# A graph kernel: four buffers in place of three for adjacency tiles, four in place of two for row loads, and a new order of the steps

## What is computed

```
h = max(layernorm(x), 0)
x = x + (A / clip(sum(A, axis=2), 1)) @ h            # layer 0: weighted mean over neighbors
h = max(layernorm(x), 0)
neigh = (A > 0) without the diagonal;  rank = exclusive cumsum of neigh;  nb = neighbors of a node
skip = ceil(nb / 2) if nb > 10 else 1
rem = neigh & (skip > 1) & (rank % skip == skip - 1) & mask;  rem = rem | rem.T
nd  = remaining neighbors and the node itself
agg = 0.25 * q25 + 0.5 * q50 + 0.25 * q75 of h over nd, per node and feature   # quantiles: a sort
y   = (relu((h + agg) @ W1 + b1) @ W2 + b2) * mask
x   = x + y                                           # layer 1
```

## Time and profile before

| | us |
|---|---|
| median of 3 runs | 1412.35 |
| lowest, highest | 1406.98, 1413.56 |
| the profiled execution | 1415.25 |
| its span in the trace | 1413.4 |

### The profile page before, as it was taken

How to read it: one execution, slowest core, us unless ns; L and a number is a source line. 1 busy time by engine, 2 the same in 40 slices (tenths; PEclk the granted TensorE clock), 3 DMA queues, 4 the chain that set the end, 5 groups by cost and what they waited for, 6 DMA issues and landing times.

```text
span 1413.4 us, 29112 instructions
## 1 busy us (share of the span) xinstructions
PE 1117.8 (79%) x11217; PEld 819.7 (58%) x11217; DVE 1083.5 (77%) x1964; ACT 695.9 (49%) x1387; POOL 876.7 (62%) x1120
## 2 busy tenths in 40 slices
...
DMA packets 124660, 173.22 MB, mean 123 GB/s; under 512 B 62272, under 2 KB 63056, under 8 KB 124496
## 3 DMA queue, kind: packets, MB, share of 16 engines
...
HBM read 119.64 MB, written 51.46 MB: 121 GB/s over the span
## 4 chain that ended last, share of the span: by engine, by line
POOL 32%; PE 24%; DVE 21%; issue 12%; DMA 5%; ACT 4%; ACTq 0%; POOLq 0%; DVEq 0%; SPq 0%
PE psL L585 7%; POOL out L1671 7%; PE psG L682 5%; PE psT L596 4%; POOL rows L1629 4%; DMA rows<-VR,IDX 4%; DVE HUB L1325 3%; PE psG L673 3%; DVE HUB L1324 3%; POOL RK L1539 2%; DVE OHB L1242 2%; DVE OHB L1253 2%; POOL rows L1550 2%; ACT VR L863 2%; DVE W L1275 1%
## 5 line engine op out<-in xcount | busy, mean ns | idle before, releaser
L585 PE MATMUL psL<-H0A,AT 128*128 128x65 f32 x2048 | 292.3, 305 | 23.2 <-issue 10.8
L585 PEld LDWEIGHTS psL<-H0A,AT 128*128 128x128 f32 x2048 | 279.6, 220 | 39.3 <-issue 33.6
L596 PE MATMUL psT<-UM,NEIT 128*128 128x512 f16 (+3 forms) x1024 | 186.4, 324 | 47.9 <-POOL NEIT L1491 23.6
L1324 DVE TENSOR_TENSOR HUB<-HUB 128x1472 f32<-128x1472 f32 (+6 forms) x224 | 182.2, 814 | 41.1 <-ACT HUB L1005 37.2
L1629 POOL DMA_INDIRECT rows<-VR,IDX x128 | 161.5, 1261 | 58.5 <-issue 34.8
L682 PE MATMUL psG<-OHB,HL 128*64 128x384 f16 (+5 forms) x2048 | 181.2, 326 | 8.9 <-DVE OHB L1253 8.6
L1325 DVE TENSOR_TENSOR HUB<-HUB 128x1472 f32<-128x1472 f32 (+6 forms) x224 | 183.8, 821 | 0.0
L673 PE MATMUL psG<-OHB,HL 128*64 128x256 f16 (+1 forms) x2560 | 163.4, 287 | 13.9 <-DVE OHB L1242 12.6
L596 PEld LDWEIGHTS psT<-UM,NEIT 128*128 128x128 f16 x1024 | 93.3, 106 | 138.0 <-issue 37.1
L1671 POOL DMA_INDIRECT out<-FR x128 | 148.6, 1161 | 38.9 <-issue 36.3
L673 PEld LDWEIGHTS psG<-OHB,HL 128*64 128x64 f16 x2560 | 140.5, 119 | 32.9 <-DVE OHB L1242 16.0
...
## 6 DMA issues: line engine op xcount, KB each, us to landing
AT<-in_adjt SPq DMA_DIRECT2D x128, 512.0 KB
RR<-rows SPq DMA_DIRECT2D x128, 288.0 KB
...
rows<-VR,IDX POOLq DMA_INDIRECT x128, 5.2
out<-FR POOLq DMA_INDIRECT x128
```

The lines of the kernel that those rows point to most:

```text
L585: m = e.matmul(ps["L"][:, 65 * t:65 * t + 65], AT[:, n % RING, kk, t * P:t * P + P], H0A[:, T * b + 2 * kp + kk, :], start=(kp == kk == t ...
L596: m = e.matmul(o[:, kk * P:COLS], half(t // 4)[:, at:at + P], UM[:, 0:COLS - kk * P], start=(kk == 0), stop=(kk == 3), skip_group_check=True)
L1324: e.tensor_tensor(b0, a0, a1, ALU.max)
```

## The change

The adjacency ring `RING` has four buffers in place of three, `AT` is that much larger, and the load waits for the tile four before. The row buffer `RR` has `RB` = 4 parts in place of 2, with a semaphore for each; the load waits for the turn and the count of load `n - 4`. The count on ACT keeps its own two buffers (`JUNK`). And the string `ORDER` is another one: it has the same 2880 letters, each as often, in another sequence. No operation is added, removed or changed in size. Lines below the top of the file are two further down from the semaphores on (L1491 is L1493 there).

```diff
-RING = 3
+RING = 4
+RB = 4
 TB = 3
 ORDER = (
-    "nnMMMMXnWAAUDDDMUDMUDAADWDAMDUMRAAARDDDDUDADDADDDNAMMWgNUNUUUUMkMSUDDUUUUUAhMSSSSMSSDSDDDRADMMWDADDD"
+    "XnnUnUUMMWAAADUMMUUDADMRMAADDDDADMDDWDDDDMDAUUUDDDURNgAMMAUNMUUUUAUWhNkMSSDADDSSSASlMMDSSDUUWRHADMMA"
...
-        RR = sb("RR", [P, 2, R_X1], F16)
+        RR = sb("RR", [P, RB, R_X1], F16)
...
-        d_row, d_out, d_feat = ([sem(f"{n}{i}") for i in range(2)] for n in ("d_row", "d_out", "d_feat"))
+        d_row = [sem(f"d_row{i}") for i in range(RB)]
+        d_out, d_feat = ([sem(f"{n}{i}") for i in range(2)] for n in ("d_out", "d_feat"))
...
-                    if n >= 2:
-                        w.wait_ge(t_full, t_use("turn", filled[n - 2][0], filled[n - 2][2]) + 1)
-                        w.wait_ge(a_cn, n - 1)
-                    e.dma_start(RR[:, n % 2].bitcast(I32), rows(g, b)[rt * P:rt * P + P, 0:R_X1 // 2]).then_inc(d_row[n % 2], 16)
+                    if n >= RB:
+                        w.wait_ge(t_full, t_use("turn", filled[n - RB][0], filled[n - RB][2]) + 1)
+                        w.wait_ge(a_cn, n - RB + 1)
+                    e.dma_start(RR[:, n % RB].bitcast(I32), rows(g, b)[rt * P:rt * P + P, 0:R_X1 // 2]).then_inc(d_row[n % RB], 16)
...
             def positions_up(g, b, rt):
                 n = nth["ldr", g, b, rt]
-                w.wait_ge(d_row[n % 2], 16 * (n // 2 + 1))
+                w.wait_ge(d_row[n % RB], 16 * (n // RB + 1))
...
             def valid(g, b, rt):
                 n = nth["cn", g, b, rt]
-                w.wait_ge(d_row[n % 2], 16 * (n // 2 + 1))
+                w.wait_ge(d_row[n % RB], 16 * (n // RB + 1))
```

More of the change, by code:

```diff
@@ new lines @@
+    "XnnUnUUMMWAAADUMMUUDADMRMAADDDDADMDDWDDDDMDAUUUDDDURNgAMMAUNMUUUUAUWhNkMSSDADDSSSASlMMDSSDUUWRHADMMA"
+    "bARUDDDDADDDNDDTDDNDAAigXBUNkUUSSnnSMSMMMDHSbDSDUDSUUSWhnrcRMAMMAATDBiMMlARDALrMWDDAAFDDDUDDUfNDDDUN"
+    "DMcALNWAFFdDdcLgMFFFFFFckSSeSSLDSLeSdDmmmmdcVMAmRdDMmFLMDUhFeddUeAAASSlLUDMmdFfULcLVRcdmmmdeDNDmdcdW"
+    "DDmKUNUDKDdADcHAXDUmtLDDmeDNdDDndmcFeAcAdmmLdLgnTFWdkUbFFSSScFndSmLScMFdSMiLdeSfembcSFBmKFectMcDMDGd"
+    "FvtrDLDvmDAAdTtDFLRmAoGMWDtdBDtFFaUimAKmDeFtDMUKptMMUDDeHddrUpRDpMMMmtKtDcQDKthDULKmUpDQKQFFcWQFgAtA"
@@ new lines @@
+    "DAftpFlFUQcFQtALFFNtdLpedLUcNMtQkmmdSLLmSSScNQUhFUStRAQDSMMLtVdUSLJQtQKJcDmdQASetdJtWAAJUDtUUDDJMpRM"
+    "QDetltmLFedmtUQDDNDQpTtdAANHmLXQDAdcDDFmtQcDDmDUiNdenDdtDQWDmQgtnFcmcQbdQFLdQkeASSnQmLQLmFMdmMMMQUdS"
+    "ccQKSESKUEBKSdReDddSFKADmmDddKLbEMmeFmEDeEeAAUSUFrFcmDVTitBMFDGKWrAEddDEDmteEGHEFcLLFUUKccmtFmFLLdDD"
+    "WvMdtAvEDLDtDDAetFaLdDReomMDmKDFMmtDcMEdmtAhclKtegFFpkFQMNFFUptQJLQFANUSScMQKSSctFDNUDLUULdAQSmQSSdR"
+    "QUtMSMQmtdcAhmtAtULDWLpDAtJMUcDttMltHQDDDQDQdJOFmteQJDDDDUdALRdtFNetmpmbdJAtNDmFXfLpDeDtdcQQOmTNFdQD"
@@ new lines @@
+    "dtnmQgWeFQdDQLmntAcQnpectmdifKkptQMMmSStpDdcQVSAUKUSQQQUVASLFMQUdDDUDQMSDEDLmBADdDHKbASeFdScKULmemEW"
+    "crFmLdmcUFAEUTRDdDtDEMKeddmDmeDDFFFMcmEUmMKdeicEAcBdFKeMmFEtdRAFDDDmtdMWdvArtdtlDgEmvLhAmEmoEEtkFFLN"
+    "SQcStMMNcLFFSFQMtpNASUtKFFFKLApODcFQRDKtLcMLUDpDQScphtdltDMJeepQADdLSSUULUUtJMMQHtALDDtQSmmRtDWFDNQO"
+    "tJQtGQQtWdNFmXQtJedtmQUdcLcDdLAcLemtcDQAtmQQDDDTGNDedmUmfJtdndFeDmDQAngdQtbemcmUpFdpQiKntdVAktUKpttQ"
+    "SSQQSQaMBfFLmdMmLSSHQdUQmSSScdAQErKFeFDMLdtmeDbKeUmTDUcFKmdLFdDEFdEemdemcMKDcRKdDtiAmFDdMtGcMKAdFFUm"
@@ new lines @@
+    "UcVBmMvMdtRLUtvFDArEomEctEmEEMWFEdtdLLDAEeEDKLDtcheeQOmmMQtQFDDDltMcFDNMDFQtLgDJtFLFQFFQNQtFDQLQFctK"
+    "UGcAUQQmAddmWLNQdchctAkcepdLtSSdtFlSmSFSSdbSpUmtJedptAmFDDSRptDDmLQUdADOMtMMMJaLtJtJUtQAtdHmeDmXRmAf"
+    "DtLQNdDdDQmNQWtpNDtUADQDnDtQDdUnUUUUDTpDDDQneQAieQKdMmLpdmMQApgQBAkQdmFSQKWSmMSEFLMeSDrSUmSDFfKLRAed"
+    "mKdcFtdFVDeSmeDddccKHFmAEUDSAEdKmMmeDEDEFALcDEbEctMFcDMdUDcFmtWicFLtdvTUUtmLLDBDFeDdMADFEtRKDmcmEMrt"
+    "dEvFKDgMDtdDtoVehmKltLmcUkpNFAEWQUAMFNSpFQLecQbFAMANSSpFSQthFDQRJMSpQtcQFAQQJtDQKtcDpFtSSdJDtMpttSLL"
@@ new lines @@
+    "DOFmDLAtdpUUtdtDMAtMQJmDDUWcQmGeRDDmAldtNQDLTtQAJeWFDHDUOdXmdNUmQQtcmcdFUDAmNdtndLtAdfDeDDmcQUicQdmg"
+    "eeFtnFQdtQnQVaQQGQdkpQSdQLUSSBmLMMmSLfEdKmKFSSLdAUMdmUeDcmVDmSdeecFAcEdmELemMtEFmbFESDRDFrdFHKDmeMcE"
+    "AcDMddADWFtLctUmKEFdiTKtdBDtmerEMGFDEvmdEFFtvLEUKmDDomtMDmROhKpdpGtpQltFKFFQDKDAFtDLQKeMcFcDNDLQAUQt"
+    "NMcpeLFQQFtFpDQOQtdhmJQNAtLQLLMUdcMQctAJgQJmdtFkmptSedcdStmJFUFtpWUULSDmeAdmSAJDfdQtDQtScfRtdlDeLQLS"
+    "mmDcmStdtdtUAmeDQQdmAtSdVVetaLLmQHtKMtbDpcDQQdDcTMmQQQcDdKQWdMFQEMDLLRDDieDmDEmNDLdDetKDNmddNFgFBdFe"
@@ L58 @@
+    "FcmkSGKFmLdGEESKmcedbecmcSSKcESSvFvStESroEtmdTHtdtFtpFtiFtKBmELEteKptEpptptQFFQrQEtFmKdQQmtctQcteQdt"
+    "cdFFttFmmeFhOOFcQtKJFQFFpQQlcJtFmddmFmcQtedJdJQdLtFdmQmtmQtLddeJQmeVtemQQmddttQccLLtdFQpmcQpLaeLFFQQ"
+    "cdVQmFdLFQdmLmdmQEmmmeKddcecKEdtdmFeFcdKcemKfdEmeEKKctcKdEvEtEmvKFFotEFdpmKeptdFQmtQQtQKpFtdptEQmQQt"
+    "QQtGmdtQtQetmQtepJQJtpEpJQGEQJtJQtQQttttOtQttttttLLOQQQQQpQLaQEEEEEEEEELEOEfLLOL"
 )
```

34 lines of the change are left out of this document (3 added, 31 removed).

## The result

The changed kernel took 1360.95 us (median of 3 runs, 1358.59 to 1363.81) against 1412.35: a ratio of 0.965, with a 95% interval of 0.960 to 0.970. (The kernel before takes about 1412 us on some chips and 1454 on others.

What follows compares the result with a forecast made beforehand. Neither PE (79% busy) nor DVE is full; work plus waits bound it, POOL's serial steps being 32% of the chain. 1415.25 − 5.4 − 9.5 − 1.0 + 2.2 = 1401.55, so 1401.5 us; range 1385 to 1420.

Steps and rivals of the forecast that it cites:

- Rings by themselves 0: The deeper adjacency and row rings alone: 0 us; bounds 5.84 us gained for adjacency tiles, 11.1 for rows.
- The fourth buffer's real use is that it lets the order place loads earlier: Ring of row loads: taken as 0 us by itself, its use being earlier loads in the new order.
- Place A: Start, pair 1: search moved behind three operations, diagonal ahead of take-out; PE waits of 2.39 and 2.98 go, 5.4 us gained.
- Place B: Pairs 6 and 7: pair 7's diagonal ahead of hub thinning on POOL; DVE's wait goes, 9.5 us gained.
- The bound of 0: Place B: no gain if DVE's next work needs rows whose take-out ends at 1069 as before.
- no POOL-caused PE wait: Sign of being right: none near 1060, and DVE's hole there below 2 us.
- Place C: Last pair: diagonal ahead of rank step; 10.5 us added, 10.2 and 1.25 saved, sum −1.0 us; bounds +9.25 and −7.19.
- the place in pair 5: POOL's diagonal comes 7.7 us later, PE has some 5.5 us of work ahead: +2.2 us; bounds 0 and +7.7.
- Rival 1: Denser DVE holds POOL's small operations; one new hold costs 11.6 us, leaving 1413; chance 27%.
- Rival 2: Last rank step's 10.5 us stand bare; take-out 9.25 us later, end 1424.5 if holds eat A and B; chance 15%.
- last sign of being wrong: DVE's idle time in the middle changed by more than 15 us by waits that were not priced.
- Place D: The place in pair 5 where POOL's diagonal comes later; priced at +2.2 us.

Runs made afterwards that it cites:

- e1: The old order on the new rings of four buffers; ratio to the kernel before 0.9965 (0.992 to 1.001).
- e5: The changed kernel with 99 adjacency loads and 39 row loads held back towards their old start; ratio to the kernel before 0.9618 (0.955 to 0.968).
- e6: The old order with both rings of four and the edits of places A and B; ratio to the kernel before 0.9975 (0.994 to 1.001).
- e9: Both rings of four, the old order up to the first one-hots of pair 6, then the new order; ratio to the kernel before 0.9961.
- e7: The old order with both rings of four, another DVE step put between 22 pairs of adjoining sorting stages; ratio to the kernel before 1.0037.
- e10: The old order with both rings of four, three 0/1 tiles of pair 7 moved ahead of pair 6's search on DVE; ratio to the kernel before 1.0014.
- e12: Old order, both rings of four; pair 6's residual one 0/1 tile later, three of pair 7's 0/1 tiles ahead of pair 6's search; ratio 0.9988.

## Why the prediction was wrong

- **Rings by themselves 0: right.** e1 gave 0.35% at most likely, and its interval holds none. e5 shows the same from the other side. The waits for loads were slack.
- **"The fourth buffer's real use is that it lets the order place loads earlier": half right.** It lets the order put the readers in another sequence. Earlier loads alone bring nothing (e1), and holding loads back cost nothing (e5, most adjacency tiles and few rows).
- **Place A, −5.4: right by luck.** The last 0/1 tile of the next half is 5.7 us earlier, but 3.6 of them were there when pair 1's messages began. SP's queue, which the working left out, stands in the way in e6, which has A and B in the old order and measured nothing.
- **Place B, −9.5: wrong as priced.** The wait went and the coefficients, 2 us behind, took its place (e6, and 6.51 us in the changed kernel). The bound of 0 was the right end. The sign "no POOL-caused PE wait" failed with it, and DVE's longest idle time there is 2.46 us and not below 2.
- **Place C, −1.0, and the place in pair 5, +2.2:** inside the noise. In C the rank step held POOL's list up by 5.8 us and not 10.5. PE's wait in pair 5 is the same, 6.47 us. The last take-out ended 184.5 us from the end of the span before and 177.5 after; within 3 us was forecast.
- **Rival 1** (new holds on POOL) did not come: the longest fell from 11.92 to 6.40 us. Its rule was read too simply: the cast did not last "exactly while" DVE ran without a gap, for that run went on for 11.7 us behind the cast, and with DVE idle 59 us less the holds became shorter. **Rival 2** has its place in the trace (12.6 us from classes to place list), but its cost is not to be seen in e9.
- **The step that failed** is the last of the sum: "DVE idles 147 us of the 950 between 200 and 1150, and I expect as much in new waits". It idled 115, 32 us less, which is the prediction's own last sign of being wrong (more than 15 us). The rest of the order, most of its letters, was entered at zero because its steps shift by less than 10 us each. The places that were priced brought nothing in the old order (e6), and the whole brought 3.2 to 3.4% over the rings, so this rest, alone or together with them, holds nearly all of the gain. The sum also had PE's work as fixed, where its clock and with it 17.5 us of its busy time moved.

What is shown: the gain is neither the rings nor the loads' lead, and in the old order neither places A and B nor the two holds make it. Place D was not tried. The tail from pair 6 on is worth at most a few us. The gain lies in the sequence before pair 6, and neither the part to pair 3 nor pairs 4 and 5 alone hold all of it. What is argued and not shown is why. One reason may be that the kernel has several limits close behind each other on PE, DVE and POOL (at place B less than 2 us), so taking one away hands the wait to the next (seen in e6; e7 and e10 to e12 fit it), while a sequence that moves all engines' steps together takes idle time from all of them at once: 59 us on DVE, 37 on PE and 46 on POOL. A rival that no run tests is PE's clock: in the new order PE was granted the higher level for more of the time (0.50 to 1.00 at place A, 405.0 to 341.5 us at the lower level in all), which shortens its work and so what waits for it. Which of the two leads, and which moves are needed together, stays open.
